# A chunked delta-rule decoder block: 2x2 and pair key products and the near fold go to GpSimd, the retrieval matmuls lose their zero columns

## The chip, the cores and the metric

The kernel runs on one core of one Trainium2 chip. The metric is the device time of one execution in microseconds (us), the median of several runs. One more execution is recorded by the hardware profiler; the rows below come from it.

## What is computed

The reference is a decoder block over x of 8 sequences of 512 tokens with 256 features: a linear-attention part that updates a state per head token by token (the delta rule), then a masked softmax attention over a context, then a feed-forward part with quantised activations and ternary weights. The part that the change touches is the first:

```python
q, k, v, beta = (heads(q), heads(k), heads(v), heads(beta))       # 16 heads of 16
k = k / jnp.maximum(jnp.linalg.norm(k, axis=-1, keepdims=True), NORM_EPS)
def step(S, inp):
    q_t, k_t, v_t, beta_t = inp
    retrieval = jnp.einsum('bhij,bhj->bhi', S, k_t)
    S = S + jnp.einsum('bhi,bhj->bhij', beta_t * (v_t - retrieval), k_t)
    o_t = jnp.einsum('bhij,bhj->bhi', S, q_t)
    return (S, o_t)
_, out_t = lax.scan(step, S0, (q, k, v, beta))
```

## The kernel before

The 512 tokens are cut into 32 chunks (NCK) of 16 tokens (CT). A chunk holds 8 sequences x 16 tokens on 128 partitions, and 16 heads x 16 tokens (CW = 256) in the free direction. Each engine runs its own program, in the order in which the code issues it, with counting semaphores between them. All of it is written out by hand: the loop `for j in range(NCK + 1)` stands once in the program of each engine, and iteration j works on chunk j and prepares chunks j+1 to j+5. What an engine issues later waits behind what it issued before.

Within a chunk the 16 tokens depend on each other. VectorE (DVE) solves this triangular system in `solve` (L1272 on): the even and odd token of a pair (L1287, L1288), pairs against pairs (L1292 product, L1295 sum), 4 tokens against 4 (L1306, L1314, L1317), and in the middle 8 against 8 (L1306 on psG). The factors are inner products of the keys of the chunk: `far_products` (8x8 blocks, L1378) and `near_products` (4x4 and 2x2 blocks, L1388, and pairs, L1391) form elementwise products of keys on DVE, TensorE (PE) sums them over the 16 features of a head with `far_gram` (L1925) and `near_gram` (L1919, L1920), and `scale_near` (L1345, L1347) and `scale_pairs` (L1353, L1355) multiply them by beta on the way from PSUM into the tiles G2, G3 and G4. `fold_near` (L1363, L1365) multiplies part of G3 by G4 and adds it to another part of G3, so that one product and one sum serve a pair.

Between two chunks the state is carried in PSUM: DVE transposes the solved values (`updates_turned`, L1331), PE adds their products with the keys to the state (`state`, L1902), ScalarE (ACT) copies the state to SBUF (L701), PE applies it to the keys and queries of the next chunk (`retrieval`, L1941), and DVE starts that chunk from the result (`start_chunk`, L1402).

`retrieval` issues for each of the 16 heads four 32x32 tile matmuls. The moving operand is not only the 32 columns of the head in the chunk's own keys and queries: the tile `padded` holds zeros before and behind them, and the matmul streams all three pieces, 96 columns (64 for the first and the last head), adding zero to the neighbouring heads:

```python
a, b = 1 if h == 0 else 0, 2 if h == NH - 1 else 3
...
last = M.matmul(into[rows, h - 1 + a:h - 1 + b], scopy[rows, h, :], streams[rows, h, a:b], ...)
```

GpSimd (POOL) has in iteration j, in this order: `mask_attention` (L537) as soon as DVE has solved chunk j (u_done), the addition of the output bias to x (L596), `x_added` (L557), and the key norms of chunk j+3 (L547, L548, L550), which wait for sums that ACT copies out of PSUM (L743) behind the retrieval and `key_sums` (L2007) on PE. In some iterations there are a few small operations more.

Of the kernel before, what the change touches and what calls it, by code (L numbers as in the profile page):

```python
# [135 lines left out]
def decoder(nc, x, ctx, mask, ln_g, ln_b, w_qkvb, b_qkvb, w_out, b_out, x_gamma, x_beta,  # L136
# [8 lines left out]
    with ExitStack() as stack:  # L145
# [74 lines left out]
        scopy = sexp_flat[:, 0:NH * 2 * HD].rearrange("p (h n) -> p h n", h=NH)  # L220
        zeros = kexp_flat[:, 0:NH * 2 * HD]
        wq_s = wq_flat.rearrange("p (c n) -> p c n", c=DC)
        bb_s = take(D)
# [87 lines left out]
        def few(n, dt=F32, rows=P):  # L311
# [71 lines left out]
             "h_ready h_last habs_ready cand_taken").split()]  # L383

        found, edge_marked, marks_summed = sem("found"), sem("edge_marked"), sem("marks_summed")
        part = [sem(f"part{k}") for k in range(2)]
# [100 lines left out]
        def _(pool):  # L487
# [85 lines left out]
            def late_inputs(k):  # L573
# [12 lines left out]
                G.tensor_scalar(f[:, 0, :], f[:, 0, :], 1.0, None, ALU.add).then_inc(stat_ready, 1)  # L586

            own(G.memset(half, -0.5))
            for m in range(3):
                key_norms(m)  # L590
            pool.wait_ge(wo_in, 32)
            for j in range(NCK):
                pool.wait_ge(u_done, j + 1)
                mask_attention(j)
                pool.wait_ge(xr_ready, j + 1)
                G.tensor_tensor(xc[:, j, :], xc[:, j, :], bb_s, ALU.add).then_inc(xb_ready, 1)  # L596
                if j >= 1:
                    x_added(j - 1)
                if j + 3 < NCK:
                    key_norms(j + 3)  # L600
                if j in FACTORS_AT:
                    late_inputs(FACTORS_AT[j])
                if j in ROW_NORMS_AT:
                    row_norms(ROW_NORMS_AT[j])
                if 12 <= j < 16:
                    for p in range(2 * (j - 12), 2 * (j - 12) + 2):
                        bounded_weights(p)
# [84 lines left out]
        def _(act):  # L692
# [29 lines left out]
            def attention_out(j, f):  # L722
                act.wait_ge(att_mm, 2 * j + 2)
                if f == 0 and j >= 1:
                    act.wait_ge(o_mm, j - 1)
                A.activation(attn[j % 2][:, f * 512:(f + 1) * 512], ps[(2, 0)[f]][:, :], ACT.Copy).then_inc(att_out, 1)  # L726

            def keys(m):
# [299 lines left out]
            for j in range(NCK + 1):  # L1028
# [5 lines left out]
                if j >= 1 and exists(j):  # L1034
                    state(j)
                if exists(j - 1):
                    updates_turned(j - 1)
# [135 lines left out]
        def _(v):  # L1173
# [100 lines left out]
            def solve(j, between):  # L1274
# [6 lines left out]
                for t in range(1, CT):  # L1281
# [7 lines left out]
                    elif t % 4 == 2:  # L1289
                        a = t // 4  # L1290
                        part = prod[:, 0:NH * 8].rearrange("p (h t s) -> p h t s", t=2, s=4)
                        own(V.tensor_tensor(part, g3h[:, :, a].rearrange("p h (t s) -> p h t s", s=4),  # L1292
# [57 lines left out]
            def scale_pairs(m):  # L1350

                bt = beta[m % 4]
                own.issue(V.tensor_tensor(G4, psG[:, 768:896], bt.rearrange("p (q t) -> p q t", t=2)[:, :, 1], ALU.mult))  # L1353
                odd = "p (q a) -> p q a"
                V.tensor_tensor(g3[:, :, 1, 2], psG[:, 768:896].rearrange(odd, a=2)[:, :, 1],  # L1355
                                bt.rearrange("p (q t) -> p q t", t=4)[:, :, 3], ALU.mult).then_inc(pre2, 1)
# [24 lines left out]
            def near_products(m):  # L1381
# [4 lines left out]
                for n, first in ((4, 1024), (2, 1536)):  # L1386
                    key = kq[m % 4][:, 0:CW].rearrange("p (q t) -> p q t", t=2 * n)
                    V.tensor_tensor(PR[:, first:first + 16 * 8 * n].rearrange("p (q t s) -> p q t s", t=n, s=n),  # L1388
                                    over_s(later_keys(m, 2 * n)[:, :, n:2 * n], n), over_t(key[:, :, 0:n], n), ALU.mult)
                key = kq[m % 4][:, 0:CW].rearrange("p (q t) -> p q t", t=2)  # L1390
# [130 lines left out]
            for j in range(NCK + 1):  # L1521
# [21 lines left out]
                if exists(j + 2):  # L1543
                    far_products(j + 2)
                    near_products(j + 2)
                if exists(j + 1):
                    fold_near(j + 1)
                if exists(j + 1):
# [323 lines left out]
        def _(pe):  # L1872
# [42 lines left out]
            def near_gram(m):  # L1915
                pe.wait_ge(prod2, m + 1)
                if m >= 1:
                    pe.wait_ge(far_used, m)
# [9 lines left out]
            def retrieval(m):  # L1928
# [6 lines left out]
                for h in range(NH):  # L1935
                    if h % (NH // 2) == 0:
                        pe.wait_ge(state_copied, 2 * m - 1 + h // (NH // 2))
                    a, b = 1 if h == 0 else 0, 2 if h == NH - 1 else 3
                    for r in range(4):
                        rows = slice(32 * r, 32 * r + 32)  # L1940
                        last = M.matmul(into[rows, h - 1 + a:h - 1 + b], scopy[rows, h, :], streams[rows, h, a:b],  # L1941
                                        start=False, stop=True, skip_group_check=True)
# [215 lines left out]
            for j in range(NCK + 1):  # L2158
# [17 lines left out]
                if j == NCK:  # L2176
# [3 lines left out]
                    context_whole(1, 1)  # L2180
                    pe.wait_ge(ctxT_ready, 4)
                if exists(j):
                    attention(j, 0)
                    far_gram(j, 0)
                    far_gram(j, 1)
                    attention(j, 1)
                if exists(j - 1):
# [177 lines left out]
```

## Time and profile before

| | |
|---|---|
| median of 3 runs | 910.58 us (910.43 to 911.65) |
| profiled execution, its own time | 912.2 us |
| its span, first to last instruction | 910.1 us |
| mean granted TensorE clock | 0.952 of full speed |
| PE busy | 786.4 us (86%) |
| DVE busy | 763.6 us (84%) |
| ACT busy | 567.7 us (62%) |
| POOL busy | 439.8 us (48%) |

The chunk loop fills the span from about 45 to 560 us; what follows is the softmax attention and the feed-forward part. Busy times are unions of intervals; a matmul in fp32 is recorded as two MATMUL instructions, so the 64 matmuls of a retrieval are 128 records. An engine's idle time is given in front of the instruction that ended it, with the instruction that released it.

### The profile page before, as it was taken

How to read it: one execution, taken by the hardware profiler on the slowest of the kernel's cores; microseconds unless marked ns; L12 is line 12 of the kernel's file. 1: busy time of each engine (PE TensorE's matmuls, PEld its weight loads, DVE VectorE, ACT ScalarE, POOL GpSimd, SP SyncE). 2: the span in 40 equal slices, each digit the busy share in tenths (PEclk: the TensorE clock that was granted, in tenths of full speed). 3: DMA queues.
4: the chain of work that ended last, by engine and by line, in shares of the span. 5: the costliest groups of instructions: out<-in, count | busy, mean ns of one | idle time of the engine just before them, and what ended most of it. 6: DMA issues, size and time to landing. Idle time of an engine off the chain costs nothing.

```text
span 910.1 us, 31226 instructions
## 1 busy us (share of the span) xinstructions
PE 786.4 (86%) x12291; PEld 583.0 (64%) x12291; DVE 763.6 (84%) x2383; ACT 567.7 (62%) x1505; POOL 439.8 (48%) x472
## 2 busy tenths in 40 slices
PE   7799999999999999999999998799999506994385
PEld 7477777777777777777777776466666304442364
DVE  3789999999988999899899986566777786999897
ACT  4576777765766666667566644357777533993294
POOL 5346546643454545434435433548788733950000
PEclk9899999999999999999999999999999956997599
DMA  9800000000000000022000001432200000000023
GB/s 185 158 2 15 9 11 13 8 14 10 10 14 8 12 12 8 13 86 73 14 9 12 12 8 37 145 133 76 71 1 1 1 0 1 1 1 1 0 80 106
DMA packets 28616, 31.24 MB, mean 34 GB/s; under 512 B 5548, under 2 KB 23864, under 8 KB 28472
## 3 DMA queue, kind: packets, MB, share of 16 engines
q1 hardware_dynamic: 28256, 29.12, 12.1%
q8 instruction: 98, 1.61, 0.8%
q14 instruction: 46, 0.38, 0.1%
q10 hardware_dynamic: 216, 0.14, 0.1%
HBM read 20.85 MB, written 4.19 MB: 28 GB/s over the span
## 4 chain that ended last, share of the span: by engine, by line
DVE 48%; PE 42%; issue 6%; ACT 2%; POOL 1%; DVEq 0%; ACTq 0%; POOLq 0%
DVE arena L1306 7%; DVE arena L1314 7%; PE psY L1941 5%; PE ps L2096 4%; PE psX L1941 4%; DVE arena L1292 4%; DVE arena L1295 4%; PE ps L1902 3%; PE psX L2117 3%; DVE arena L1288 3%; DVE arena L1287 3%; DVE arena L1317 3%; PE psY L2117 2%; PE ps L2302 2%; PE psG L2096 2%
## 5 line engine op out<-in xcount | busy, mean ns | idle before, releaser
L537 POOL TENSOR_TENSOR arena<-arena 128x1024 f32<-128x1024 f32 x32 | 75.8, 2370 | 178.3 <-DVE arena L1295 178.3
L548 POOL TENSOR_TENSOR work<-work,half 128x16 f32<-128x16 f32 x32 | 97.9, 3061 | 2.7
L1314 DVE TENSOR_REDUCE arena<-arena 128x64 f32<-128x256 f32 (+1 forms) x96 | 65.9, 687 | 3.3
L1925 PE MATMUL psG<-arena 128*128 128x512 f32 x128 | 64.7, 629 | 0.0
L726 ACT ACTIVATE arena<-ps 128x512 f32<-128x512 f32 x64 | 34.7, 594 | 46.6 <-PE ps L1967 46.4
L547 POOL TENSOR_SCALAR work<-work 128x16 f32<-128x16 f32 x32 | 8.1, 252 | 103.7 <-ACT work L743 103.7
L1976 PE MATMUL ps<-arena 128*128 128x128 f32 x384 | 49.8, 279 | 2.9 <-ACT arena L726 1.5
L1976 PE MATMUL ps<-nT,arena 128*128 128x128 f32 x384 | 49.4, 279 | 3.3 <-ACT nT L780 1.2
L1976 PEld LDWEIGHTS ps<-arena 128*128 128x128 f32 x384 | 45.7, 192 | 6.3 <-ACT arena L726 5.5
L2096 PE MATMUL ps<-arena,nT 128*128 128x512 f32 x84 | 42.7, 632 | 7.6 <-issue 5.2
L1976 PEld LDWEIGHTS ps<-nT,arena 128*128 128x128 f32 x384 | 45.2, 192 | 5.9 <-ACT arena L726 4.4
L772 ACT ACTIVATE arena<-ps,columns 128x128 f32<-128x128 f32 x64 | 20.1, 364 | 45.6 <-PE ps L1976 45.6
L1902 PEld LDWEIGHTS ps<-work 32*32 32x32 f32 x1984 | 29.9, 105 | 26.6 <-issue 26.6
L1902 PE MATMUL ps<-work 32*32 32x64 f32 x1984 | 34.0, 215 | 14.7 <-DVE work L1331 14.7
L1967 PEld LDWEIGHTS ps<-work 32*64 32x64 f32 x1024 | 27.9, 132 | 28.3 <-issue 27.5
L1131 ACT ACTIVATE arena<-ps,small 128x512 f32<-128x512 f32 x64 | 41.8, 690 | 6.5 <-PE ps L2302 5.7
L1967 PE MATMUL ps<-work 32*64 32x128 f32 x1024 | 43.5, 282 | 2.1 <-ACT arena L780 1.8
L1941 PE MATMUL psY<-work,arena 32*32 32x96 f32 (+1 forms) x2048 | 44.4, 238 | 1.0 <-issue 0.6
L962 ACT ACTIVATE arena<-arena 128x512 f32<-128x512 f32 x32 | 23.1, 721 | 33.7 <-DVE arena L1443 33.6
L1941 PEld LDWEIGHTS psY<-work,arena 32*32 32x32 f32 x2048 | 41.5, 105 | 4.1 <-issue 4.1
L1306 DVE TENSOR_TENSOR arena<-psG,arena 128x1024 f32<-128x1024 f32 x32 | 39.2, 1224 | 4.3 <-PE psG L1925 3.2
L1941 PE MATMUL psX<-work,arena 32*32 32x96 f32 (+1 forms) x1920 | 41.6, 239 | 0.0
(358 smaller groups left out, 2410.2 us busy)
## 6 DMA issues: line engine op xcount, KB each, us to landing
arena<-in_mask_BxSxS_ik SPq DMA_DIRECT2D x8, 1024.0 KB, 6.7
xs<-arena SPq DMA_DIRECT2D x256, 16.0 KB, 1.9
arena<-in_ctx SPq DMA_DIRECT2D x8, 512.0 KB, 4.2
out<-xs SPq DMA_DIRECT2D x32, 128.0 KB, 1.7
arena<-in_x SPq DMA_DIRECT2D x8, 288.0 KB, 13.4
arena<-in_L_ffn_w SPq DMA_DIRECT2D x2, 1024.0 KB, 19.0
arena<-in_x SPq DMA_DIRECT2D x16, 96.0 KB, 5.2
arena<-in_L_attn_w_qkvb SPq DMA_DIRECT2D x2, 512.0 KB, 5.3
```

The source lines that it names most:

```text
L537: G.tensor_tensor(keys, keys, same_half.rearrange("p (a t) -> p a t", a=1).broadcast_to([P, NH, HALF]), ALU.mult).then_inc(att_masked, 1)
L548: own(G.tensor_tensor(root, length, half, ALU.pow))
L1131: A.activation(gT[:, n * 512:(n + 1) * 512], ps[n % 3][:, :], ACT.Gelu, scale=deq[:, 0:1]).then_inc(gabs, 1)
L1306: mult = V.tensor_tensor(part, src, C16[:, :, t - n:t].rearrange("p h (a s) -> p h a s", a=1).broadcast_to([P, NH, n, n]), ALU.mult)
L1314: own(V.tensor_reduce(sums, part, AX.X, ALU.add))
L1902: last = M.matmul(psS[rows, b * 64:b * 64 + 64], kt[rows, b * 32:b * 32 + 32], utm[rows, b * 64:b * 64 + 64], start=False, stop=True, skip ...
L1925: M.matmul(psG[:, f * 512:(f + 1) * 512], block16[:, :], PF[m % 2][:, f * 512:(f + 1) * 512], start=True, stop=True).then_inc(g1_mm, 1)
L1941: last = M.matmul(into[rows, h - 1 + a:h - 1 + b], scopy[rows, h, :], streams[rows, h, a:b], start=False, stop=True, skip_group_check=True)
L1967: last = M.matmul(ps[(2, 0)[r % 2]][tokens, first:first + P].rearrange("p (e t) -> p e t", e=2), kq[j % 4][rows, f * P + HALF * u:f * P + ...
L1976: last = M.matmul(out[:, f * P:(f + 1) * P], wq_s[:, c, first:first + P], nT[m % 4][:, c, :], start=c == 0, stop=c == DC - 1)
L2096: last = M.matmul(logit_bank(n), nT[n % 2][:, c, :], ctxT[b % 2][:, c, :], start=c == 0, stop=c == DC - 1)
L2117: last = M.matmul(psO[n % 2], probT[n % 2][:, u * P:(u + 1) * P], ctx_s[b % 4][:, u, :], start=u == 0, stop=u == NW - 1)
```

## The change

Five edits, none of which changes the result:

1. `near_products` for chunks 2 and later issues on DVE only the 4x4 products; the 2x2 products and the pair products are formed by a new function `small_products` on POOL, which reads both factors from SBUF. `near_gram` on PE waits for both.
2. `fold_near` for chunks 1 and later moves from DVE to POOL, with a tile of its own (`folded`) for the product. DVE waits for it inside `solve`, ahead of the first L1292 of the chunk.
3. The second instruction of `scale_pairs` (L1355), which writes the scaled pair factor into G3, becomes a copy out of G4 on ACT, `pairs_copied_over`, behind the copies of the state.
4. The matmuls of `retrieval` stream only the head's own 32 columns.
5. In iteration 0 alone PE issues `far_gram` ahead of the first part of `attention`.

```diff
+            def small_products(m):
+                pool.wait_ge(g2_mm, m)
+                pool.wait_ge(k_ready, m + 1)
+                key = kq[m % 4][:, 0:CW].rearrange("p (q t) -> p q t", t=4)
+                shape = [P, key.shape[1], 2, 2]
+                G.tensor_tensor(PR[:, 1536:1792].rearrange("p (q t s) -> p q t s", t=2, s=2),
+                                key[:, :, 2:4].rearrange("p q (t a) -> p q t a", a=1).broadcast_to(shape),
+                                key[:, :, 0:2].rearrange("p q (a s) -> p q a s", a=1).broadcast_to(shape), ALU.mult)
+                key = kq[m % 4][:, 0:CW].rearrange("p (q t) -> p q t", t=2)
+                G.tensor_tensor(PR[:, 1792:1920], key[:, :, 1], key[:, :, 0], ALU.mult).then_inc(prod3, 1)
+            def fold_near(m):
+                pool.wait_ge(pre2, m + 1)
+                pairs = folded.rearrange("p (q s) -> p q s", s=2)
+                G.tensor_tensor(pairs, g3[:, :, 0, 0:2],
+                                G4.rearrange("p (q a b) -> p q a b", a=2, b=1)[:, :, 1].broadcast_to([P, NH * 4, 2]),
+                                ALU.mult).then_inc(folds, 1)
+                pool.wait_ge(folds, m)
+                G.tensor_tensor(g3[:, :, 1, 0:2], g3[:, :, 1, 0:2], pairs, ALU.add).then_inc(near_folded, 1)
...
                 mask_attention(j)
+                if j + 2 < NCK:
+                    small_products(j + 2)
+                if j + 1 < NCK:
+                    fold_near(j + 1)
                 pool.wait_ge(xr_ready, j + 1)
...
+            def pairs_copied_over(m):
+                act.wait_ge(pre2, m + 1)
+                A.activation(G3.rearrange("p (q t s) -> p q t s", t=2, s=4)[:, :, 1, 2],
+                             G4.rearrange("p (q a) -> p q a", a=2)[:, :, 1], ACT.Copy).then_inc(pairs_copied, 1)
...
                     state(j)
+                    pairs_copied_over(j)
...
+                        if t == 2 and j >= 1:
+                            v.wait_ge(near_folded, j)
+                            v.wait_ge(pairs_copied, j)
...
                 if exists(j + 1):
-                    fold_near(j + 1)
-                if exists(j + 1):
                     start_chunk(j + 1)
...
             def near_gram(m):
                 pe.wait_ge(prod2, m + 1)
+                if m >= 2:
+                    pe.wait_ge(prod3, m - 1)
...
-                    a, b = 1 if h == 0 else 0, 2 if h == NH - 1 else 3
...
-                        last = M.matmul(into[rows, h - 1 + a:h - 1 + b], scopy[rows, h, :], streams[rows, h, a:b],
+                        last = M.matmul(into[rows, h], scopy[rows, h, :], streams[rows, h, 1],
```

POOL, one iteration of the chunk loop, before; the names in brackets are the semaphores that the instruction waits for:

```order
L537 TENSOR_TENSOR arena<-arena 128x1024 [waits att_out,u_done]
L596 TENSOR_TENSOR arena<-arena 128x256 [waits xr_ready]
L557 TENSOR_TENSOR arena<-arena 128x256 [waits xb_ready,mixed_out]
L547 TENSOR_SCALAR work<-work 128x16 [waits seeded]
```

The same iteration now. All line numbers have moved: L540 is the mask, L625 the bias, L560 `x_added`, L550 to L553 the key norms.

```order
L540 TENSOR_TENSOR arena<-arena 128x1024 [waits att_out,u_done]
L597 TENSOR_TENSOR arena<-work 128x256 [waits k_ready,g2_mm]
L601 TENSOR_TENSOR arena<-work 128x128
L607 TENSOR_TENSOR arena<-arena 128x128 [waits pre2]
L611 TENSOR_TENSOR arena<-arena 128x64x2 [waits folds]
L625 TENSOR_TENSOR arena<-arena 128x256 [waits xr_ready]
L560 TENSOR_TENSOR arena<-arena 128x256 [waits xb_ready,mixed_out]
L550 TENSOR_SCALAR work<-work 128x16 [waits seeded]
L551 TENSOR_TENSOR work<-work,half 128x16 [waits pool_chain]
L553 COPY work<-work 128x256 [waits rn_T,pool_chain]
```

The four new instructions stand between the mask and the two additions to x, and ahead of the key norms.

DVE between two chunks, now, from the transposes to the last products (of before, the rows are in the section below: L1355, the second L1388, L1391, L1363 and L1365 have no counterpart here):

```order
L1370 STREAM_TRANSPOSE work<-arena 128x256 [waits s_mm,u_done]
L1370 STREAM_TRANSPOSE work<-arena 128x256
L1365 TENSOR_TENSOR work<-work,ps 128x256 [waits kraw_ready,rn_T]
L1384 TENSOR_TENSOR arena<-psG,arena 128x512 [waits beta_ready,g2_mm]
L1386 TENSOR_TENSOR arena<-psG,arena 128x128x2
L1441 STREAM_TRANSPOSE work<-work 128x256 [waits s_mm]
L1393 TENSOR_TENSOR arena<-psG,arena 128x128
L1421 TENSOR_TENSOR arena<-ps,work 128x1024 [waits key_copied,g1_mm,k_ready]
L1431 TENSOR_TENSOR arena<-ps,work 128x512 [waits key_copied,k_ready,g2_mm]
```

Behind these rows `start_chunk` follows at once.

## Rows read from the trace of the kernel before

**Rows 1.** The page, part 2: granted clock in 40 slices of the span.
```profile
PEclk9899999999999999999999999999999956997599
```
**Rows 2.** Waits from 100 to 540 us: who waited for whom, us in total, times, longest.
```profile
PE ps L1902 <- DVE work L1331: 12.3, 26, 0.7
DVE arena L1402 <- PE psY L1941: 6.4, 13, 1.3
DVE arena L1402 <- PE psX L1941: 5.6, 13, 0.6
```
**Rows 3.** Chain that ended last, between two chunks: start us, us, what.
```profile
261.30 0.46 DVE work L1331
...
261.89 1.10 PE ps L1902 x64
...
264.46 2.78 PE psX L1941 x125
267.24 0.03 issue
267.27 0.62 DVE arena L1402 x2
...
277.79 0.46 DVE work L1331
```
**Rows 4.** Timeline of DVE, same stretch: start, duration, line, tiles, shape, count.
```profile
263.75 0.26 DVE L1355 TENSOR_TENSOR arena<-psG,arena 128x64 f32<-128x64 f32 x1
263.92 1.22 DVE L1378 TENSOR_TENSOR arena<-ps,work 128x1024 f32<-128x1024 f32 x1
265.05 1.01 DVE L1388 TENSOR_TENSOR arena<-ps,work 128x512 f32<-128x512 f32 x2
266.49 0.29 DVE L1365 TENSOR_TENSOR arena<-arena 128x128 f32<-128x128 f32 x1
268.35 0.29 DVE L1292 TENSOR_TENSOR arena<-arena 128x128 f32<-128x128 f32 x1
```
**Rows 5.** Groups of DVE by shape from 60 to 541 us: busy us, mean ns.
```profile
L1388 DVE TENSOR_TENSOR arena<-ps,work 128x512 f32<-128x512 f32 x29 | 19.6, 676 | 0.0
```
**Rows 6.** Groups of PE by shape, 60 to 541 us; then timeline of PE around 264 us.
```profile
L1902 PE MATMUL ps<-work 32*32 32x64 f32 x1856 | 31.8, 215 | 13.8 <-DVE work L1331 13.8
L1941 PE MATMUL psX<-work,arena 32*32 32x96 f32 x1680 | 37.8, 241 | 0.0
...
264.39 2.82 PE L1941 MATMUL psX<-work,arena 32*32 32x64 f32 x128
```
**Rows 7.** Timeline of ACT, same stretch.
```profile
263.04 1.14 ACT L701 ACTIVATE arena<-ps,nparity 128x128 f32<-128x128 f32 x4 [0.25 <-PE ps L1902]
265.63 0.81 ACT L780 ACTIVATE nT<-ps,columns 128x128 f32<-128x128 f32 x2
```
**Rows 8.** Timeline of POOL, same stretch.
```profile
261.35 2.36 POOL L537 TENSOR_TENSOR arena<-arena 128x1024 f32<-128x1024 f32 x1 [4.52 <-DVE arena L1295]
263.66 0.73 POOL L596 TENSOR_TENSOR arena<-arena 128x256 f32<-128x256 f32 x1
264.35 0.73 POOL L557 TENSOR_TENSOR arena<-arena 128x256 f32<-128x256 f32 x1
268.39 3.04 POOL L548 TENSOR_TENSOR work<-work,half 128x16 f32<-128x16 f32 x1
```
**Rows 9.** Timeline of DVE and POOL around the start of chunk 31.
```profile
541.53 2.36 POOL L537 TENSOR_TENSOR arena<-arena 128x1024 f32<-128x1024 f32 x1 [12.50 <-DVE arena L1295]
543.58 0.46 DVE L1363 TENSOR_TENSOR arena<-arena 128x128 f32<-128x128 f32 x1
543.86 0.77 POOL L596 TENSOR_TENSOR arena<-arena 128x256 f32<-128x256 f32 x1
544.07 0.70 DVE L1365 TENSOR_TENSOR arena<-arena 128x128 f32<-128x128 f32 x1
```
**Rows 10.** Timeline of PE in chunk 0: `far_gram` at the lower clock.
```profile
33.65 3.25 PE L1925 MATMUL psG<-arena 128*128 128x512 f32 x4
```

More of the change, by code:

```diff
@@ L221, in decoder @@
         zeros = kexp_flat[:, 0:NH * 2 * HD]
+        folded = kexp_flat[:, NH * 2 * HD:NH * 2 * HD + P]
         wq_s = wq_flat.rearrange("p (c n) -> p c n", c=DC)
@@ L383, in decoder @@
              "h_ready h_last habs_ready cand_taken").split()]
+        folds, near_folded, pairs_copied = sem("folds"), sem("near_folded"), sem("pairs_copied")
+        prod3 = sem("prod3")
         found, edge_marked, marks_summed = sem("found"), sem("edge_marked"), sem("marks_summed")
@@ L1352, in scale_pairs @@
                 bt = beta[m % 4]
+                if m >= 1:
+                    V.tensor_tensor(G4, psG[:, 768:896], bt.rearrange("p (q t) -> p q t", t=2)[:, :, 1],
+                                    ALU.mult).then_inc(pre2, 1)
+                    return
                 own.issue(V.tensor_tensor(G4, psG[:, 768:896], bt.rearrange("p (q t) -> p q t", t=2)[:, :, 1], ALU.mult))
@@ L1387, in near_products @@
                     key = kq[m % 4][:, 0:CW].rearrange("p (q t) -> p q t", t=2 * n)
-                    V.tensor_tensor(PR[:, first:first + 16 * 8 * n].rearrange("p (q t s) -> p q t s", t=n, s=n),
-                                    over_s(later_keys(m, 2 * n)[:, :, n:2 * n], n), over_t(key[:, :, 0:n], n), ALU.mult)
+                    last = V.tensor_tensor(PR[:, first:first + 16 * 8 * n].rearrange("p (q t s) -> p q t s", t=n, s=n),
+                                           over_s(later_keys(m, 2 * n)[:, :, n:2 * n], n), over_t(key[:, :, 0:n], n), ALU.mult)
+                    if m >= 2:
+                        last.then_inc(prod2, 1)
+                        return
                 key = kq[m % 4][:, 0:CW].rearrange("p (q t) -> p q t", t=2)
@@ L1916, in near_gram @@
                 pe.wait_ge(prod2, m + 1)
+                if m >= 2:
+                    pe.wait_ge(prod3, m - 1)
                 if m >= 1:
@@ L2181, in _ @@
                     pe.wait_ge(ctxT_ready, 4)
+                if j == 0:
+                    far_gram(j, 0)
+                    far_gram(j, 1)
                 if exists(j):
                     attention(j, 0)
+                if exists(j) and j >= 1:
                     far_gram(j, 0)
                     far_gram(j, 1)
+                if exists(j):
                     attention(j, 1)
```

## The prediction

> **What bounds the kernel now.** I read the page first: the granted clock is at its upper level through all of the chunk loop, slices 3 to 24 [rows 1]. Then the waits: in the loop nearly every wait on the path is between two engines. PE waits for DVE's transposes 12.3 us in 26 chunks, 0.47 us each, and DVE waits for the retrieval 6.4 + 5.6 us in 26, 0.46 us each [rows 2]. Both engines are otherwise full, so a gain on one alone is worth at most the other's slack. The chain shows how they meet [rows 3]. It leaves DVE at L1331 (261.30), runs over PE's state and retrieval, and is back on DVE at L1402 (267.27): 5.97 us. From there to the next L1331 (277.79) it is DVE alone, 10.52 us of `solve`. The period is their sum, 16.49 us.
>
> Beside PE's 5.97 us DVE works from 261.30 until L1365 ends at 266.49 + 0.29 = 266.78 [rows 4], 5.48 us. So between the two meetings there are two nearly equal paths, PE's and DVE's. The change shortens both, and brings in a third, POOL's.
>
> **DVE's part.** Gone are L1355, the second L1388, L1391 and both folds. L1355 costs its pitch, 263.92 - 263.75 = 0.17 us. Of the L1388 pair the 4x4 one stays, 0.68 us [rows 5]; it would end at 265.05 + 0.68 = 265.73 where L1365 ended at 266.78, so 1.05 us go. In sum 1.22 us: DVE is ready for L1402 at 265.56, 4.26 us behind L1331.
>
> **PE's part.** The retrieval is 128 records, begun at 264.39, lasting 2.82 us; less the 0.24 us that one takes [rows 6], 2.58 us over 127 steps are 20.3 ns each, for 92 columns on average (112 of 96, 16 of 64). The state's 64 records of 64 columns take 1.10 us [rows 3], less 0.215 [rows 6]: 14.0 ns each. Time per column is 0.221 and 0.219 ns: both are bound by columns, and 32 columns would then be 7.0 ns. No row shows so narrow a tile matmul. Bounds: 14.0 ns (32 columns are not dearer than 64 on the same tiles), and 7.0 ns. I take 9 ns, near the lower, since the two rows show no fixed part. Then the retrieval takes 127 x 9 ns + 0.22 = 1.36 us and DVE could start L1402 at 264.39 + 1.36 + 0.03 = 265.78; with 14.0 ns at 266.42, with 7.0 at 265.53. It is not held earlier: ACT's copies of the state end at 263.04 + 1.14 = 264.18 [rows 7].
>
> The Trainium skill, page "TensorE: Matmul & The Clock Gate", section "Back-to-back issue gap", has a floor of about 25 ns between matmul starts, the same for 1 to 64 columns. By it 127 steps would cost 3.2 us, more than the 2.58 that 92 columns take, and edit 4 would give nothing. The trace does not show this floor on row tiles: 14.0 ns.
>
> **POOL's part.** This is where the change costs. The mask starts at 261.35 and the next instruction at 263.66 [rows 8]. A product of 1024 columns takes 2.36 us and a sum of 256 takes 0.73: 2.12 ns a column on 0.19 us fixed [rows 8]. 128 columns are then 0.46 us. Instructions follow each other 0.04 us before the recorded end (263.66 + 0.73 against 264.35). The four new ones put 0.69 + 0.42 + 0.54 + 0.42 = 2.07 us in between (the third has a wait of 0.08 us on its own result, my estimate from the gap ahead of such waits). So L596 starts at 265.73, L557 at 266.42 and ends at 267.15. The fold is ready at about 265.8, L1292 needs it at 267 or later: hidden. Not shown is what patterns with inner runs of two cost POOL; bounds are nothing extra, and twice the column part of the four (2.12 ns x 640 = 1.36 us more). I take nothing, since the mask's factor is also a repeated pattern and fits the line.
>
> **Where POOL meets DVE.** Chunk 31 has no far and near products, so DVE reaches its two folds while POOL is still busy [rows 9]. L1363 starts at 543.58 and takes 0.46 us, where L1365, of the same shape, takes 0.29 in the earlier chunk [rows 4]: it ends 0.15 behind the mask (543.89). L1365 takes 0.70 and ends at 544.77, 0.14 behind L596 (544.63). So a DVE operation with both inputs in SBUF stands until a POOL operation on SBUF ends. Operations with an input in PSUM are not slowed: L1378 takes its 1.22 us beside L557 [rows 4, 8]. Before, POOL's additions end at 265.08 and `solve` begins behind them. Now `solve` meets them.
>
> The Trainium skill, page "SBUF — State Buffer", section "Who interferes with whom", says it as a rule: such a DVE instruction and a GpSimd instruction that reads SBUF exclude each other for the whole instruction. Chunk 31 agrees. It would also stop `solve` for the 3.04 us of L548; there the trace disagrees (L1292 at 268.35 takes its 0.29 us).
>
> **The sum.** L1402's two instructions take 0.61 + 0.03 us, so L1287 comes at 266.42, at the end of L596. Either it slips through between the additions and L1288 is held, or it is held itself, until 267.15 + 0.15 = 267.30. L1292 then starts between 267.35 and 267.55, where it started at 268.35: 0.8 to 1.0 us per chunk, taken as 0.88. It depends little on the retrieval: with 14.0 ns L1287 comes at 267.06 and is still held to 267.30. 29 chunks (2 to 30) give 25.5 us. Chunk 1 is bound by DVE and gives its 1.1; chunk 31 waited 2.4 us for PE and gives the retrieval's 1.4. Together 28.0 us. In time of the profiled execution that is 912.2 - 28.0 = 884.2; the median is 1.6 us under that execution, so 883.
>
> Costed at nothing: the copy on ACT (about 0.26 us like L1355) is put behind 264.18, and delays what follows on ACT by no more than that; L780 ends at 266.44 [rows 7], about 266.6 then, and PE's attention part waits for it perhaps 0.2 us after an earlier retrieval. PE has room: its cycle becomes 16.49 - 0.47 - (2.58 - 1.14) = 14.6 us of a period of 15.6. If that cover went, each 0.1 us would be 3 us in all. POOL's key norms wait for sums that leave PE behind the retrieval; POOL is free for them at 267.15, and began L548 at 268.39 so far [rows 8]. `near_gram` waits for products that POOL finished a chunk earlier. Edit 5 touches chunk 0 only.
>
> **The rivals.**
> - POOL's narrow operations are dear. At the upper bound L557 ends 1.36 us later, at 268.5, and L1292 starts at 268.7 or later instead of 268.35: no gain. Half of it gives 0.2 to 0.3 us a chunk, 903 us. For it: no row shows such a pattern; against: all adds fit one line. Chance 0.15, of which 0.04 within 0.2% or slower.
> - POOL does not hold `solve` as in chunk 31 (its operations are short, or DVE goes first). Then L1287 comes at 266.42 instead of 267.91: 1.49 us a chunk, 45.7 in all, 865 us. For it L548; against rows 9. Chance 0.12.
> - The retrieval does not follow its columns: bound by the issue of its 256 instructions. At 18 ns L1402 starts at 266.9, L1292 at 268.0: 0.35 us, 900 us. With no gain at all L1402 stays, and so does the time. Against: 14.0 ns at 64 columns. Chance 0.08, of which 0.02 for no change.
> - Slower: the zeros kept PE at its upper clock, and without them it falls in the loop. Chunk 0 shows the price: four records of 512 columns in 3.25 us [rows 10], where at the loop's rate (four tiles at once, so 4 x 0.22 ns a column) they would take 1.8. If the stretch from state to retrieval (now 3.9 us) runs at the lower level, L1402 comes 3.9 us later than forecast and the chunk loses 2.4 us instead of gaining 0.88. It decides from 27% of the chunks; at half of them the kernel takes about 933 us. For it: PE will wait about 0.9 us a chunk instead of 0.47. Against: waits of up to 0.7 us left the clock at its upper level [rows 1, 2]. Chance 0.05.
>
> **How the numbers follow.** The forecast keeps 0.60: 875 to 892. To hold 8 in 10, the range takes in part of the dear-POOL and slow-retrieval cases above and of the free-POOL case below: 872 to 899. A measurement tells 0.2% (1.8 us) from no change. Faster: 0.60 + 0.12 + 0.11 + 0.06 = 0.89; same 0.03; slower 0.05 + 0.03 = 0.08.
>
> **What would show it.** L1941's successor at 1.2 to 1.5 us for 128 records instead of 2.82; the four POOL instructions at 0.73, 0.46, 0.46, 0.46; the first L1287 or L1288 of a chunk at 0.4 to 0.9 us instead of 0.19, ending 0.15 behind POOL's second addition; the period at 15.6 us; DVE's wait ahead of L1402 near 0.2 us; the clock unchanged. I am wrong if POOL's four take over 2.6 us, if DVE is not held, or if the clock falls.

## The result, and the profile after

The changed kernel takes 899.1 us in the median (four runs, 895.03 to 910.74) where the one before took 910.5 beside it: a ratio of 0.9858, 95% interval 0.9829 to 0.9886. Run again later, unaltered, it took 893.4 us (887.97 to 904.14), ratio 0.9804 (0.9756 to 0.9851). Ratios leave out executions that lie over 1.5% above the fastest of the same kernel, here 910.74. The other three have a median of 896.7 us. So the change makes it faster by 1.4 to 2%, and 899.1 lies just above the high end of the range; the forecast was 883. The distance of 0.1 us from the range is well within the scatter of the runs, and 893.4 lies inside it: what decides is the mechanism, below.

The profiled execution lasted 901.5 us where that of before lasted 912.2; the spans, 899.6 and 910.1, differ by 10.5 us. The page after:

```profile
span 899.6 us, 31249 instructions
...
PE 766.8 (85%) x12284; PEld 552.7 (61%) x12291; DVE 730.6 (81%) x2230; ACT 572.0 (64%) x1536; POOL 493.1 (55%) x594
...
PEclk9999799999996999996999999999999857997599
```

DVE is 33 us less busy, POOL 53 us more. The line of the clock answers to [rows 1]: in slices 5, 13 and 19, all in the loop, it is now at 6 or 7 tenths.

Where the 10.5 us come from is read off the first transposes of DVE behind a chunk (L1331 before, L1370 now). They mark the period of the loop. Timeline of DVE after, first and last chunk boundary:

```profile
41.54 0.77 DVE L1370 STREAM_TRANSPOSE work<-arena 128x256 f32<-128x256 f32 x2
...
535.15 0.77 DVE L1370 STREAM_TRANSPOSE work<-arena 128x256 f32<-128x256 f32 x2
```

Before they stood at 44.65 and 541.49. So 3.1 us were gained ahead of the loop, 3.2 in its 30 periods (496.8 to 493.6 us), and 4.2 behind it. The last part was not changed. It took 368.6 us before and 364.5 after, and 365.7 to 370.3 us in all other traces below but one (379.0), so I count it as scatter. The loop gave 3.2 us where 28 were forecast. This is the slowest of the three executions that count; a second trace of the same kernel, of 892.42 us, is read further down, and there the loop gave 14.1.

It is not that every chunk gained little. In an undisturbed chunk, called ordinary from here on, the period fell from 16.40 to 15.38 us, by 1.02. Before, most chunks kept this pace (median 16.41); now five of the 30 do, and the median is 15.83. All 30 at 15.38 would have given 30.6 us. But seven of them last 17.88 to 19.37 us, in sum 23.4 us over 7 x 15.38, and the rest 8.8 over it. Before, the same excess was 496.8 - 30 x 16.40 = 4.8 us. So 27.4 us of 30.6 are given back.

A chunk of 15.38 us, timeline of PE. The columns are start, duration, engine, line, operation, tiles, shape, count, and in brackets the idle time ahead and its releaser:

```profile
189.52 1.09 PE L1946 MATMUL ps<-work 32*32 32x64 f32 x64 [0.47 <-DVE work L1370]
...
192.03 0.90 PE L1986 MATMUL psX<-work,arena 32*32 32x32 f32 x82
193.14 0.59 PE L1986 MATMUL psX<-work,arena 32*32 32x32 f32 x46 [0.21 <-issue]
```

The retrieval runs at (0.90 - 0.20)/81 = 8.6 ns a record, and even here it stands once, for "issue": neither data nor a semaphore is missing. Without a stall the 128 records last 1.29 us. The timeline of POOL beside it, which answers to [rows 8]:

```profile
188.98 2.37 POOL L540 TENSOR_TENSOR arena<-arena 128x1024 f32<-128x1024 f32 x1 [5.93 <-DVE arena L1334]
191.31 0.62 POOL L597 TENSOR_TENSOR arena<-work 128x256 f32<-128x256 f32 x1
191.88 0.40 POOL L601 TENSOR_TENSOR arena<-work 128x128 f32<-128x128 f32 x1
192.23 0.46 POOL L607 TENSOR_TENSOR arena<-arena 128x128 f32<-128x128 f32 x1
192.77 0.46 POOL L611 TENSOR_TENSOR arena<-arena 128x128 f32<-128x128 f32 x1
193.18 0.72 POOL L625 TENSOR_TENSOR arena<-arena 128x256 f32<-128x256 f32 x1
193.86 0.72 POOL L560 TENSOR_TENSOR arena<-arena 128x256 f32<-128x256 f32 x1
```

The four new ones take 193.18 - 191.31 = 1.87 us in all.

And one of the seven bad chunks, timeline of PE, then of DVE:

```profile
269.87 1.25 PE L1986 MATMUL psY<-work,arena 32*32 32x32 f32 x124
272.85 0.25 PE L1986 MATMUL psY<-work,arena 32*32 32x32 f32 x4 [1.73 <-issue]
...
274.76 3.78 PE L1971 MATMUL psG<-arena 128*128 128x512 f32 x4
```
```profile
278.65 1.23 DVE L1345 TENSOR_TENSOR arena<-psG,arena 128x1024 f32<-128x1024 f32 x1 [1.56 <-PE psG L1971]
...
290.31 0.42 DVE L1365 TENSOR_TENSOR work<-work,ps 128x256 f32<-128x256 f32 x1 [4.36 <-ACT arena L770]
```

PE stands for 1.73 us within the retrieval, with nothing to wait for but its instructions. Then the four far Gram records last 3.78 us (1.98 in the chunk before), and up to 290.3 the granted clock averages 0.61. DVE, which in the loop before waited for nothing but the retrieval [rows 2], waits for both. The waits of 100 to 540 us that answer to [rows 2], some of them:

```profile
DVE work L1365 <- ACT arena L770: 15.2, 6, 4.5
...
DVE arena L1448 <- PE psY L1986: 12.0, 12, 2.7
...
DVE arena L1345 <- PE psG L1971: 9.6, 7, 3.7
...
DVE arena L1448 <- PE psX L1986: 7.1, 9, 2.5
...
PE psY L1986 <- issue: 6.3, 9, 1.7
PE psX L1986 <- issue: 4.7, 7, 2.1
PE ps L2012 <- issue: 3.8, 3, 2.1
```

Two things are new, then: stalls of PE for instructions, and a falling clock. In what follows "stalls" are the waits of PE's matmuls put down to issue from 45 to 550 us (before 0.9 us in 2 of them, now 17.2 in 22), and "low clock" is the time at the lower of the two levels from 45 to 530 us, twice the loss of the mean granted clock (before none, now 51 us in seven spells). The windows of that stretch, before and after (us, busy time of PE, PEld, DVE, ACT, POOL with instructions, clock, DMA share, GB/s):

```profile
45.00:530.00 485.00, 465.47 (x10098) 361.18 (x10100) 441.13 (x1233) 324.40 (x1024) 240.79 (x214) 1.00 0.06 17
```
```profile
45.00:530.00 485.00, 450.99 (x10179) 332.31 (x10178) 414.13 (x1098) 329.20 (x1053) 291.66 (x333) 0.95 0.07 17
```

That these stalls are a lack of instructions can be read off the DMA packets. Part 3 of the page has a queue of kind "instruction":

```profile
q8 instruction: 98, 1.61, 0.8%
```

Each of its packets has 16384 bytes. All 22 stalls end 1.1 to 1.6 us behind the landing of such a packet, and 2.4 to 2.9 us behind its start. The stall above ends at 272.85; its packet starts at 270.24, when the retrieval has begun, and lands at 271.55. At 1.29 us the retrieval uses up its instructions before the next packet is there; with 2.8 us, as before, it stood in one chunk.

### The profile page after: what moved, and what is told of

Its sections match the earlier page's. It is cut to its first block, busy times and chain, and to the rows that moved or that the text cites. A ratio compares the mean times of both kernels' runs of the same rounds, so it can differ in the third digit from the quotient of the medians.

```text
span 899.6 us, 31249 instructions
## 1 busy us (share of the span) xinstructions
PE 766.8 (85%) x12284; PEld 552.7 (61%) x12291; DVE 730.6 (81%) x2230; ACT 572.0 (64%) x1536; POOL 493.1 (55%) x594
## 4 chain that ended last, share of the span: by engine, by line
PE 46%; DVE 41%; issue 8%; ACT 4%; POOL 1%; DVEq 0%; ACTq 0%; POOLq 0%
DVE arena L1345 5%; DVE arena L1353 5%; PE ps L2141 4%; PE ps L2021 4%; PE psG L1971 3%; DVE arena L1331 3%; PE ps L1946 3%; PE psX L2162 3%; DVE arena L1334 3%; PE psY L2162 2%; PE ps L2352 2%; PE psG L2141 2%; DVE arena L1323 2%; DVE arena L1324 2%; DVE arena L1356 2%
## 5 line engine op out<-in xcount | busy, mean ns | idle before, releaser
L540 POOL TENSOR_TENSOR arena<-arena 128x1024 f32<-128x1024 f32 x32 | 75.8, 2369 | 177.2 <-DVE arena L1334 171.7
L1971 PE MATMUL psG<-arena 128*128 128x512 f32 x128 | 73.5, 703 | 0.0
L2021 PE MATMUL ps<-arena 128*128 128x128 f32 x384 | 52.7, 289 | 2.4 <-ACT arena L755 1.3
L2012 PEld LDWEIGHTS ps<-work 32*64 32x64 f32 x1024 | 29.7, 139 | 36.6 <-issue 34.5
L2021 PEld LDWEIGHTS ps<-arena 128*128 128x128 f32 x384 | 48.4, 201 | 5.7 <-ACT arena L755 4.6
L2012 PE MATMUL ps<-work 32*64 32x128 f32 x1024 | 46.6, 294 | 5.3 <-issue 3.8
L1345 DVE TENSOR_TENSOR arena<-psG,arena 128x1024 f32<-128x1024 f32 x32 | 39.2, 1224 | 10.5 <-PE psG L1971 9.6
L1965 PE MATMUL psG<-arena 128*128 128x512 f32 x64 | 39.8, 706 | 2.6 <-issue 1.8
L1331 DVE TENSOR_TENSOR arena<-arena 128x128 f32<-128x128 f32 x128 | 37.5, 293 | 4.4
L1334 DVE TENSOR_REDUCE arena<-arena 128x32 f32<-128x128 f32 x128 | 36.6, 286 | 4.4
L2352 PE MATMUL ps<-work 128*128 128x512 bf16 x124 | 37.2, 379 | 1.6 <-ACT work L1162 1.4
```

Of the source, the lines that this page charges most:

```text
L540: G.tensor_tensor(keys, keys, same_half.rearrange("p (a t) -> p a t", a=1).broadcast_to([P, NH, HALF]), ALU.mult).then_inc(att_masked, 1)
L1334: last = V.tensor_reduce(C16[:, :, t:t + 2], part, AX.X, ALU.add)
L1345: mult = V.tensor_tensor(part, src, C16[:, :, t - n:t].rearrange("p h (a s) -> p h a s", a=1).broadcast_to([P, NH, n, n]), ALU.mult)
L1971: M.matmul(psG[:, f * 512:(f + 1) * 512], block16[:, :], PF[m % 2][:, f * 512:(f + 1) * 512], start=True, stop=True).then_inc(g1_mm, 1)
L2012: last = M.matmul(ps[(2, 0)[r % 2]][tokens, first:first + P].rearrange("p (e t) -> p e t", e=2), kq[j % 4][rows, f * P + HALF * u:f * P + ...
L2021: last = M.matmul(out[:, f * P:(f + 1) * P], wq_s[:, c, first:first + P], nT[m % 4][:, c, :], start=c == 0, stop=c == DC - 1)
```

## The experiments

Theory A: the narrow retrieval (edit 4) brings both. Its 256 instructions (128 matmul records and as many weight loads) leave in 1.3 us, faster than instructions arrive, and the time that PE stands lets its clock fall. The rival, theory B: edits 1 to 3 bring them by new waits between the engines. Theories C and D, on the clock alone, stand in the expectations.

**The zeros back.** The changed kernel with edit 4 alone undone:

```diff
-  last = M.matmul(into[rows, h], scopy[rows, h, :], streams[rows, h, 1],
+  last = M.matmul(into[rows, h - 1 + a:h - 1 + b], scopy[rows, h, :], streams[rows, h, a:b],
```

> The changed kernel with the zero columns back in the retrieval (edit 4 undone). Theory A (the retrieval's 256 instructions now run faster than PE's instructions arrive; PE stands for lack of instructions, and that idle time lets its clock fall): with 92 columns on average the stalls and the spells at the lower clock go, the path over PE is 5.97 us again and bounds every chunk, period 16.4 us; about 907 us, of which 3 us less than before come from chunk 0. Theory B (the work on POOL and ACT makes PE wait and lets the clock fall): spells remain, 900 us or more with periods of 18 to 19 us in some chunks.

907.32 us (ratio 0.9937, 0.9905 to 0.997). Stalls 0.5 us in 2, no low clock, a steady period of 16.40. Groups of PE from 60 to 535 us, first of the changed kernel, then of this one; behind the second bar is the idle time ahead of them:

```profile
L1986 PE MATMUL psX<-work,arena 32*32 32x32 f32 x1920 | 21.1, 193 | 5.2 <-issue 5.2
L1986 PE MATMUL psY<-work,arena 32*32 32x32 f32 x1792 | 20.1, 194 | 6.7 <-issue 6.7
```
```profile
L1987 PE MATMUL psX<-work,arena 32*32 32x96 f32 x1680 | 37.4, 241 | 0.0
```

Both faults come with edit 4, and so does the gain per chunk: edits 1 to 3 without it leave the period where it was.

**Edit 4 alone**, in the kernel before:

> The kernel before with edit 4 alone: only the 32 own columns in the retrieval. Theory A: stalls of 0.2 to 2 us ahead of or within the retrieval and spells at the lower clock as in the changed kernel; a clean chunk takes 16.0 us (DVE's own path of 5.48 us), in all 897 to 912 us. Theory B: no spells, 16.0 us in every chunk, 896 to 898 us.

Two of its four executions took 935.53 and 937.94 us; the other two, 919.07 and 924.36, are still 7 and 12 us above the 912.11 of the kernel before. So it is slower, which I had not expected. The ordinary period is 15.9, but there are stalls (11.5 us in 18) and 20 spells of low clock (72 us in all), and the mean is 17.0. Timeline of PE:

```profile
132.78 0.82 PE L1940 MATMUL psX<-work,arena 32*32 32x32 f32 x72
134.19 0.68 PE L1940 MATMUL psX<-work,arena 32*32 32x32 f32 x56 [0.59 <-issue]
135.12 0.61 PE L2006 MATMUL ps<-arena 128*128 128x8 f32 x4 [0.26 <-DVE arena L1391]
...
136.49 3.40 PE L1925 MATMUL psG<-arena 128*128 128x512 f32 x4
```

Here PE stands twice: for instructions, then for DVE's near products, which end later than an early retrieval. Behind such a wait for DVE's near products (L1391) begin 19 of the 20 spells, within 1.4 us. Edits 1 to 3 take that second wait away. They are worth little alone and much beside edit 4.

**Two pieces instead of one or three.** The changed kernel streaming the head's own 32 columns and the zero piece behind them (64 columns), the slice being `streams[rows, h, 1:b]`:

> The changed kernel with one of the two zero pieces back: 64 columns in the retrieval (32 for the last head), as many instructions as before, each at 14.0 instead of 8 ns. DVE could start at 5.1 us behind the transposes, and POOL holds it to about the same point anyway. Theory A: hardly any stall, no or few spells, period 15.4 to 15.6 us, 882 to 888 us, faster than both kernels. Theory C (the clock falls because PE waits 0.9 us a chunk for DVE, whatever the stalls): spells as in the changed kernel, 893 us or more.

891.74 us (0.9799, 0.9755 to 0.9843). Stalls 5.1 us in 7, low clock 3.4 us; the ordinary period is 15.61 and the mean 15.89. This is 4 us slower than I had expected at most, but theory C, by which the clock would fall as in the changed kernel whatever the stalls, does not hold: one spell is left, behind a stall of 1.2 us. In the chunk shown the retrieval is one piece. It lasts 2.08 us here and 1.94 in most chunks, 0.65 longer than at 32 columns:

```profile
139.15 2.08 PE L1987 MATMUL psY<-work,arena 32*32 32x64 f32 x128
```

**Half the instructions.** The changed kernel with `for h in range(0, NH, 2)` in `retrieval`; it leaves out the retrieval of the odd heads.

> The changed kernel with the retrieval of the odd heads left out (128 instead of 256 instructions, 32 columns each; the state's share in the odd heads' outputs is missing, nothing else). Theory A: no stall of over 0.5 us in the retrieval, few or no spells, period 15.3 to 15.5 us. Theory C or a clock that falls for want of columns: at least as many spells as in the changed kernel, since PE has less work still. Where other values send the later quantile search on another way, only the chunk loop is compared.

883.31 us (0.971, 0.966 to 0.9761). No stall is longer than 0.6 us, 3.7 us in all; yet the low clock is 34 us, and the mean period 15.69 over an ordinary one of 15.14. So a lack of instructions is not needed for the clock to fall. But idle time there is: six of the eight spells begin 1.4 to 2.1 us behind a wait of 0.6 to 0.9 us for DVE's near products, which the still shorter retrieval outruns, and the other two behind stalls of 0.4 and 0.6 us.

**Wide work to hold the clock.** Two matmuls of 128 zero columns over the whole array, added to the changed kernel behind each retrieval, and then in its middle:

```diff
+  for _ in range(2):
+      M.matmul(psR[...][:, 0:P], zeros[:, 0:P], zeros[:, 0:P], start=False, stop=True, ...)
```

> The changed kernel with two matmuls of 128 zero columns on the full array behind each retrieval (they add zero to a bank that PE owns), 0.43 us of column work in 8 records. It does nothing for the instruction stalls within the retrieval. Theory D (the clock falls where the short retrieval, its stalls and the narrow key sums leave too little column work close together): fewer spells than in the changed kernel, stalls as many; 885 to 893 us. Theory A alone (stalls are the whole cause): spells and time as in the changed kernel, 895 to 901 us.

> The changed kernel with the same two matmuls between the two halves of the retrieval: the 256 instructions no longer come in one run, at the price of 0.43 us on the path to the next chunk. Theory A and D: stalls shorter, spells rare; period 15.5 to 15.8 us, 885 to 892 us, about as the kernel with one zero piece. If neither stalls nor column work matter: 0.3 us a chunk slower than the changed kernel, 905 us.

Behind: 895.86 us (0.9811, 0.9764 to 0.9858), no different from the changed kernel in either of its measurements. Its only trace is of its slowest execution, 908.48 us, and isn't used, so theory D stays open. Between: 905.92 us (0.9945, 0.9916 to 0.9974), worse. Stalls are still 12 us in 15, the low clock is 31 us, and the ordinary chunk is 0.35 us longer. Neither gained time.

**Two pieces in the kernel before**, and **two pieces with edit 5 undone:**

> The kernel before with one of the two zero pieces left out, 64 columns. It measures what the work moved to POOL and ACT is worth, against the changed kernel with 64 columns. PE's path falls from 5.97 to 5.2 us, DVE's of 5.48 us becomes the bound: period 16.0 us if the clock stays up, 0.985 of the kernel before. If the clock also needs the POOL edits' shape or all three pieces, it falls as with 32 columns and the time is at or above the kernel before.

> The changed kernel with 64 columns and with edit 5 undone (in chunk 0 far_gram again behind the first part of attention). Edit 5 was costed at nothing. The traces since show chunk 1 starting 3.1 us earlier with it: if that is edit 5, this one takes 3 to 4 us more than the kernel with 64 columns and edit 5, 0.984 of the kernel before; if the 3 us come from elsewhere, the same as that kernel.

903.59 us (0.9907, 0.9873 to 0.994) and 896.39 us (0.9834, 0.9807 to 0.9861). The first shows that a retrieval of 64 columns gains on its own (period 15.90 in ordinary chunks), and edits 1, 2, 3 and 5 some 10 us more (0.9799 against 0.9907). The second prices edit 5. Its 4.7 us of median are within scatter, but the first transposes tell it: without edit 5 they start at 44.19 here against 40.79 with it (the two kernels differ in nothing else), and in the other traces at 44.0 to 44.65 without and at 40.3 to 41.7 with it, but for one at 43.35 (additions late, below). That is some 3.3 us. The timeline of PE after shows why:

```profile
31.13 1.88 PE L1971 MATMUL psG<-arena 128*128 128x512 f32 x4
```

Before, these records ran at 33.65 at the lower clock, 3.25 us long [rows 10], and DVE's first 8x8 product waited for them until 37.00. Now that product starts at 33.89, as soon as DVE reaches it.

**The changed kernel once more, and the hold by POOL.** The changed kernel unaltered; then three edits of the two-piece version: `key_norms` ahead of POOL's two additions to x; `turn(m + 3)` on PE moved into the middle of the retrieval; and both.

> The changed kernel once more, unaltered, for a direct comparison on one chip with the three below. Stalls for lack of instructions within the retrieval and spells at the lower clock as in its first trace; 0.983 to 0.989 of the kernel before, with a wider spread than the kernels with 64 columns.

> The changed kernel with 64 columns in the retrieval, and POOL's two additions to x moved behind the key norms, where DVE works on operands in PSUM or sums. It takes POOL's hold away from the start of solve. With 64 columns the retrieval ends behind POOL's additions, so the hold should be worth little here: the period stays 15.6 us and the time 0.980 of the kernel before. If the hold still counts, 0.2 us a chunk, 6 us, 0.973.

> The changed kernel with 64 columns, and the two transposes of the normed x (turn) moved from ahead of the retrieval into its middle. No instruction more; the 256 of the retrieval are parted by four wide ones. If the run of small instructions is what outpaces their arrival, stalls are shorter and fewer, at 0.980 or a little less; if only the number of instructions per microsecond over the whole stretch counts, no difference.

> The changed kernel with 64 columns and both of these moves, as the candidate for the fastest: 0.97 to 0.98 of the kernel before, period 15.4 to 15.6 us, clock at its upper level through the chunk loop.

| | median | ratio | ordinary chunk |
|---|---|---|---|
| changed, again | 893.40 | 0.9804 (0.9756 to 0.9851) | 15.37 |
| additions late | 896.11 | 0.983 (0.9794 to 0.9865) | 15.61 |
| turn between | 899.55 | 0.9879 (0.9844 to 0.9915) | 15.94 |
| both | 900.59 | 0.9888 (0.9858 to 0.9917) | 15.94 |

The two-piece version (0.9799) can't be told from the changed kernel in time; only its trace is steadier. The last two missed what was expected of them: with the turn between, stalls are 7.9 us in 10 instead of 5 in 7, no shorter, and both together were to reach 0.97 to 0.98. Taking POOL's additions away from the start of `solve` brings nothing at 64 columns. Cutting a run of 32x32 tiles with full-array work costs 0.33 us a chunk here and 0.35 above, where the two wide matmuls themselves account for part. None of the versions beats the changed kernel for certain.

The new trace of the changed kernel, of an execution of 892.42 us, parts the two faults. Its stalls are as before, 17.9 us in 24, but the low clock is 27 us instead of 51, and the 30 periods take 482.8 us instead of 493.6. The stall of 1.73 us stands at the very same record, four before the end of the retrieval, but here the clock stays up. Timeline of PE:

```profile
270.99 0.25 PE L1986 MATMUL psY<-work,arena 32*32 32x32 f32 x4 [1.73 <-issue]
...
272.31 1.98 PE L1971 MATMUL psG<-arena 128*128 128x512 f32 x4
```

The windows over this chunk and the next, first of the trace with the spell (13.7 us), then of this one:

```profile
266.77:304.38 37.61, 34.91 (x685) 25.24 (x684) 27.76 (x75) 22.20 (x68) 20.73 (x24) 0.82 0.04 10
```
```profile
264.92:297.16 32.24, 28.96 (x685) 21.82 (x684) 28.12 (x74) 22.45 (x69) 20.90 (x24) 1.00 0.05 11
```

So that spell cost 5.4 us, 0.39 for each us at the lower level; over the whole loop it is 10.8 us for 24 us, 0.45. The stall by itself made its chunk 16.86 us long instead of 15.38. In both traces every spell, 12 in all, begins around a stall of 0.4 to 3.0 us, from 0.9 us before its end to 2.0 behind it; other stalls of up to 1.7 us brought none.

**A stall by itself.** The kernel before, with PE held behind the retrieval in chunks 5, 9, 13, 17, 21 and 25 until POOL has done a small power that begins at the retrieval's end:

```diff
+  if j + 1 in HELD:
+      pool.wait_ge(ret_mm, j + 2)
+      G.tensor_tensor(<spare 128x8>, ones[:, 0:8], half[:, 0:8], ALU.pow).then_inc(held, 1)
...
+  if j in HELD:
+      pe.wait_ge(held, HELD.index(j) + 1)
```

> The kernel before, unchanged but for six chunks (5, 9, 13, 17, 21, 25) in which PE is held behind the retrieval until POOL has done a 1.65 us operation that begins when the retrieval has ended. PE stands some 1.8 us there, as in the longest stalls of the changed kernel, with all the zero columns in place. If a stall alone brings the lower clock, most of the six are followed by a spell, and these chunks take 18 us or more; if narrow columns are needed too, no spell, and the chunk takes 17.5 to 18 us for the wait alone. In all 915 to 925 us.

933.28 us (two runs; 1.0227, 1.0136 to 1.0318). I had expected 915 to 925. Low clock 27 us, where the kernel before has none. Three of the six holds are followed by a spell (10.2 us from 120.8, 3.4 from 393.9, 13.7 from 462.2), three by none. Timeline of PE at the first:

```profile
118.67 0.61 PE L2013 MATMUL ps<-arena 128*128 128x8 f32 x4 [1.84 <-POOL arena L603]
...
119.80 2.81 PE L1931 MATMUL psG<-arena 128*128 128x512 f32 x4
```

The clock falls within those four records. The retrieval was as wide as before, so 1.8 us of idle PE is enough, sometimes.

**More instructions, the same columns.** The kernel before, each matmul of 96 columns parted into three of 32:

```diff
-  last = M.matmul(into[rows, h - 1 + a:h - 1 + b], ..., streams[rows, h, a:b], ...)
+  for z in range(a, b):
+      last = M.matmul(into[rows, h - 1 + z], ..., streams[rows, h, z], ...)
```

> The kernel before with each retrieval matmul of 96 columns parted into three of 32, the same columns in 736 records for weights and as many again instead of 128: three times the instructions for the same column work. If the pace of 8 ns is all that limits, the retrieval's stream takes 368 x 8 = 2.9 us as against 2.6 and the kernel about 0.3 us a chunk more, 920 us, without stalls. If instructions arrive more slowly than that, PE stands several us in every chunk: 950 us or more.

(The expectation counts the records wrongly: they are 368 for weights and 368 for matmuls.) 1211.67 us (two runs; 1.3278, 1.3148 to 1.3408), a mean period of 26.1. Timeline of PE:

```profile
204.32 3.39 PE L1942 MATMUL psY<-work,arena 32*32 32x32 f32 x203
209.27 2.50 PE L1942 MATMUL psY<-work,arena 32*32 32x32 f32 x128 [1.55 <-issue]
213.27 1.01 PE L1942 MATMUL psY<-work,arena 32*32 32x32 f32 x37 [1.50 <-issue]
```

This is the clearest sight of the lack. From one stall to the next there are exactly 128 matmul records, which with their weight loads are 256, and 213.27 - 209.27 = 4.00 us. In the other chunks, too, two stalls in a row are 254 to 256 records apart, and 3.5 to 4.0 us. A packet of 16384 bytes lands 1.2 to 1.6 us ahead of the end of each of them, as in the changed kernel. Once PE has used up what was fetched ahead, then, instructions come in blocks of 256, one in 3.5 to 4.0 us. Over the whole run the matmuls of the retrieval wait 69.3 us for issue, 61 times; the rest of the 300 us are a longer retrieval (15.8 ns a record at the upper clock, where the changed kernel has 8.6; why was not tried) and the lower clock, 382 us of the 817 from 45 to 862.

The Trainium skill, page "Runtime: NRT & Kernel Launch", section "Instruction fetch mechanics", has the blocks of 256 instructions, and the trace agrees. It also holds that fetching is hidden, since an engine dispatches slower than its memory is filled; here 61 stalls of 1.1 us on average say otherwise.

## Why the prediction was wrong, point by point

- **What bounds the kernel:** right. The period is still PE's path and `solve`; both engines shed what was said, and the ordinary chunk gained 1.02 us, not 0.88. The surplus is in POOL's four new operations, 1.87 us instead of 2.07, so that the last addition ends 5.60 us behind the mask's start instead of 5.80, and in DVE passing 0.04 us behind it, not 0.15. But only five chunks of 30 reached this pace.
- **The width of the retrieval:** the pace was right, 8.6 ns a record for 9, and 1.29 us for 1.36 where nothing interrupts it. The floor of 25 ns of "TensorE: Matmul & The Clock Gate", "Back-to-back issue gap", in the Trainium skill, does not show on row tiles at 32 columns either.
- **Its supply:** this is the step that failed. The rival "bound by the issue of its 256 instructions" (0.08) was priced as an even 18 ns a record, and set aside because of the 14.0 ns at 64 columns. But that row holds 64 records, and the lack is not a pace: it is a store that runs empty. (That the rival named 900 us, and 899.1 came, is chance.) At 96 columns 256 instructions leave in 2.6 us and it stalled in hardly any chunk; at 32, in 1.3 us, 18 stalls took 11.9 us within the retrieval and four took 5.3 more outside it.
- **The clock:** second failure, in the same term. The fall had a chance of 0.05, argued against by waits of up to 0.7 us that left the clock up. It was weighed for waits between engines, and the stalls of up to 2.1 us were not foreseen. The 51 us at the lower level fit the seven long chunks. Which cost more can be estimated from the two traces of the changed kernel: at 0.39 to 0.45 us for each us of low clock, 20 to 23 of the 32.2 us above the ordinary pace (23.4 + 8.8) are the clock's, and the other 9 to 12 are left for the stalls. Set against the 4.8 us of the kernel before, together they make up the 27.4 given back. What brings a spell is shown in part: in the traces of the kernels with 32 columns and of the held one, PE stood shortly before every one of them. Beside a narrow retrieval 0.4 to 1 us of it was often enough, whether it waited for instructions or for DVE; beside the wide one up to 0.7 us never was, and 1.8 us in three cases of six. Why one wait brings a spell and the next, as long, does not, stays open.
- **POOL's hold:** right. In five chunks, in which the retrieval does not stall, the first L1323, 0.18 to 0.19 us elsewhere, takes 0.54 to 0.64. In the one shown it ends 0.04 behind L560 (162.84 + 0.73); timeline of DVE:

```profile
162.99 0.62 DVE L1323 TENSOR_TENSOR arena<-arena 128x16 f32<-128x16 f32 x1
```

  It sets the 15.38 us: DVE starts the chunk 4.43 us behind the transposes and is held until 5.70, and a stall of 0.2 us in the retrieval, as in the chunk of 188.93, costs nothing. Longer ones bring `solve` behind the additions anyway. Undone at 64 columns it gave nothing; at 32 it wasn't tried. The case against a hold by the power, L548, rests on an L1292 that began 0.04 us before it; the next L1292, within it (270.62, 0.29 us), bears it out.
- **The rival of dear narrow operations:** wrong. Inner runs of two cost POOL nothing: 0.46 us for 128 columns, as on the line.
- **Edit 5, costed at nothing:** wrong by 3.3 us. "Touches chunk 0 only" is true, but chunk 0 stands on the path, and its far Gram matmuls were what DVE waited for.

So the steps that failed are the supply of the retrieval's instructions, priced as an even pace and thought unlikely, and the clock, thought to stay up. In the profiled execution they took 27.4 us, against 2.6 us more from the ordinary pace, the 3.1 of edit 5 and the scatter of the rest; in the second trace of the same kernel, 16.6 (its 30 periods lie 21.4 us above 15.38 each, less the 4.8 of before).

## What to carry to other kernels

Ahead of a matmul made narrower, count the instructions as well as the columns: a stretch whose instructions leave faster than they are fetched stopped here for 0.2 to 3 us at a time, and what the shorter work gains can be lost again to the clock, which here, by the estimate above, cost more than the stalls. In a trace look at the spread of the period before its mean; a clean period with a few long ones points to supply or clock, not to the path. And columns that add zeros can be paying for something: try an intermediate width before taking them all away.

## What the runs showed of the hardware

- PE's instructions came in packets of 16384 bytes, 256 instructions (128 matmul records with their loads). PE went on 1.1 to 1.6 us behind a packet's landing, and once it had run out they came 3.5 to 4.0 us apart.
- A 32x32 tile matmul record in fp32 cost 8.6 ns at 32 columns when tiles alternate, 14.0 at 64, 20.3 at 92 (the average of a retrieval); with three records on one tile in a row, 15.8 at 32.
- 1.8 us of idle PE lowered the granted clock after three of six equal holds; spells lasted 3.4 to 13.7 us. By the two traces of the changed kernel, 1 us at the lower level cost the loop 0.39 to 0.45 us (an estimate).
- POOL's products with inner runs of two elements cost no more than plain ones: 0.46 us for 128 columns. Its power of 128x8 lasted 1.65 to 1.67 us.
